# A four-chunk, two-layer transformer kernel: PSUM banks named step by step, folds as steps of their own, products of zeros at the start, and a new step list

## The reference, cut to what matters

```
layer 0:  xn   = layernorm(x)
          attn = causal softmax attention of xn with one head: q = xn Wq, k = xn Wk (both 1024 wide), v = xn Wv, out Wo
          ffn  = mixture over the top 2 of 8 experts; an expert is relu(xn wi + bi + xn A[e] B[e]) wo + bo,
                 the gate's logits are xn gate_w + gate_b
          x1   = x + attn * silu(ffn)
layer 1:  xn1  = layernorm(x1)
          attn = causal differential attention, 16 heads, two softmaxes per head, rms norm of each head, Wo
          ffn  = the top 8 of 32 experts (silu gate, up, down, 64 wide) and a shared expert
          out  = x1 + attn * silu(ffn)
```

## Time and profile before

| | us |
|---|---|
| runs | 492.76, 493.83, 493.89 |
| profiled execution, its time | 493.67 |
| profiled execution, its span (first to last instruction) | 491.9 |
| PE busy | 455.2 (93%) |
| DVE busy | 398.6 (81%) |
| ACT busy | 281.6 (57%) |
| POOL busy | 269.6 (55%) |

### The profile page before, as it was taken

The page is one execution under the profiler, slowest core; times in us unless marked ns, Lnnn a source line. Parts: engine busy times, 40 slices in busy tenths (PEclk is TensorE's granted clock), DMA queues, the critical chain, the costliest instruction groups (busy, mean ns, idle before and its releaser), DMA issues.

```text
span 491.9 us, 8510 instructions
## 1 busy us (share of the span) xinstructions
PE 455.2 (93%) x3072; PEld 219.5 (45%) x3072; DVE 398.6 (81%) x812; ACT 281.6 (57%) x456; POOL 269.6 (55%) x237
## 2 busy tenths in 40 slices
PE   2999888889999999999999999999889998989995
PEld 2755447434444345453454444544334453423332
DVE  1634457999998988899999978978999999986785
ACT  2264673446767635738876445556776537467640
POOL 6322360235554775547763459636675865546982
PEclk9999997999999999999999999999999999999998
DMA  7900059786952710232569643025592662204201
GB/s 277 338 14 0 22 182 194 127 142 182 234 111 76 127 18 4 73 84 65 176 181 168 111 62 91 1 65 171 178 172 43 121 98 77 58 5 113 59 2 43
DMA packets 54754, 52.44 MB, mean 107 GB/s; under 512 B 5080, under 2 KB 44344, under 8 KB 54072
## 3 DMA queue, kind: packets, MB, share of 16 engines
q1 hardware_dynamic: 54712, 51.90, 44.2%
HBM read 37.47 MB, written 13.89 MB: 104 GB/s over the span
## 4 chain that ended last, share of the span: by engine, by line
PE 73%; DVE 18%; ACT 3%; issue 2%; POOLq 1%; DMA 1%; POOL 1%; SPq 0%; DVEq 0%; ACTq 0%
PE bank L785 10%; PE bank L776 9%; PE bank L797 8%; PE scores L816 8%; PE bank L871 5%; DVE nmax L1335 3%; PE scores L711 3%; PE scores L702 3%; PE scores L726 3%; PE scores L705 3%; PE scores L810 3%; PE scores L750 3%; DVE h L1311 3%; PE bank L876 2%; DVE h L1318 2%
## 5 line engine op out<-in xcount | busy, mean ns | idle before, releaser
L1136 POOL TENSOR_TENSOR gb<-gb,wb 128x512 f32<-128x512 f32 x64 | 84.3, 1318 | 94.3 <-ACT gb L1024 76.3
L1039 ACT ACTIVATE pk<-scores 128x1024 f32<-128x1024 f32 x96 | 95.3, 1023 | 38.9 <-PE scores L816 38.7
L1129 POOL TENSOR_SCALAR_AFFINE_SELECT pk<-pk 128x512 f32<-128x512 f32 (+1 forms) x96 | 82.1, 864 | 39.8 <-ACT pk L1039 39.3
L1335 DVE TENSOR_REDUCE nmax<-scores 128x8 f32<-128x1024 f32 x64 | 76.4, 1216 | 7.7 <-PE scores L816 7.0
L1021 ACT ACTIVATE gt<-bank,bgh 128x512 f32<-128x512 f32 (+1 forms) x68 | 46.7, 687 | 62.5 <-PE bank L776 50.7
L785 PE MATMUL bank<-xnt,wu 128*128 128x512 f32 x128 | 68.3, 615 | 2.3 <-DVE h L1318 2.2
L776 PE MATMUL bank<-xnt,wg 128*128 128x512 f32 x128 | 69.4, 624 | 0.0
L797 PE MATMUL bank<-h,wd 128*128 128x512 f32 x128 | 66.5, 617 | 0.0
L1311 DVE SCALAR_TENSOR_TENSOR h<-gt,gb 128x512 f32<-128x512 f32 x64 | 57.8, 903 | 3.4 <-PE bank L797 3.1
L1318 DVE SCALAR_TENSOR_TENSOR h<-bank,bu,h 128x512 f32<-128x512 f32 x64 | 48.1, 751 | 10.8 <-PE bank L785 8.8
L1140 POOL TENSOR_TENSOR orms<-oms,minus_half 128x32 f32<-128x32 f32 x8 | 44.7, 5585 | 10.3 <-DVE oms L1365 10.3
(11 more groups left out here) (262 smaller groups left out, 711.1 us busy)
## 6 DMA issues: line engine op xcount, KB each, us to landing
wb<-wt_scratch SPq DMA_DIRECT2D x64, 256.0 KB, 4.2
parts_scratch<-parts SPq DMA_DIRECT2D x16, 384.0 KB, 3.0
qa<-parts_scratch SPq DMA_DIRECT2D x32, 192.0 KB, 4.9
ka<-parts_scratch SPq DMA_DIRECT2D x32, 192.0 KB, 5.9
parts_scratch<-parts SPq DMA_DIRECT2D x16, 256.0 KB, 3.1
parts_scratch<-parts SPq DMA_DIRECT2D x16, 128.0 KB, 2.8
ha<-in_wkq SPq DMA_DIRECT2D x1, 1024.0 KB, 4.8
wb<-in_wvo SPq DMA_DIRECT2D x1, 1024.0 KB, 7.5
```

The source lines that it names most:

```text
L1039: A(dst.rearrange("p (h m) q -> p m h q", m=2), pairs[pair_of(step)][:, :, :].rearrange("p m (h q) -> p m h q", q=cols), ACT.Exp, scale=SC ...
L1129: pool.affine_select(out=dst, in_=dst, compare_op=ALU.is_ge, fill=0.0, base=0, pattern=[[0, heads], [1, P]], channel_multiplier=-1).then_i ...
L1136: pw(gb[:, c % 2, :], gb[:, c % 2, :], wb[:, k % 2, j % 2, :], ALU.mult).then_inc(s_ga_done, 1)
L1335: V.tensor_reduce(dst, src, AX, ALU.max, negate=True).then_inc(s_nmax_done, 1)
```

## The change

1. PSUM becomes one tensor of eight banks. The list names for each step the first bank that it uses (`max/0/0/0/0@1` takes banks 1 and 2, `gate/0@5` bank 5). Bank 7 stays with `down`. A step waits for whichever steps last held its banks (`holders`, `banks_free`). `gate`, `up`, `values` and the rest no longer have banks of their own.
2. The folds are steps, `foldk/0` and `foldv/0`. On PE `foldk` stands ahead of the first transposes; on ACT its copy to `mt` stands ahead of `scale0/0`.
3. DVE fills `fth` (128x512, f32) with zeros first, and PE multiplies it by itself three times into bank 7 before it waits for anything else.
4. The gate's weights lie beside the factors A in one tile `lag` (136 columns). One product per 128 tokens gives both the logits and xn A, in step `keys0`, over two banks; the 8 matmul instructions a chunk for the logits alone (L648) are gone. `keys0` now holds its banks until `um` is done, and `inner0` holds the products with `mt` and `vo`.
5. The list is new. No instruction is added or removed by that, only moved.

Core of the diff (the same renaming of banks in every engine's part is left out, as are the two lists):

```diff
+ONE_BANK = ("foldk", "foldv", "turn0", "turn1", "router1", "fin", "minus", "values", "weights1", "out1", "gate", "up")
+ACC = 7
...
+def holders(steps, first):
+
+    last, before = {}, {}
+    for step in steps:
+        if step in first:
+            banks = range(first[step], first[step] + (1 if step[0] in ONE_BANK else 2))
+            before[step] = list(dict.fromkeys(last[k] for k in banks if k in last))
+            last.update((k, step) for k in banks)
+    return before
...
-    load/0 load/1 norm0/0 scale0/0 turn0/0 norm0/1 keys0/0 router0/0 inner0/0 picks0/0 scale0/1 scores0/0 hidden0/0
+    load/0 load/1 foldk/0@5 norm0/0 scale0/0 norm0/1 turn0/0@1 keys0/0@3 foldv/0@2 router0/0 scale0/1 inner0/0@5
...
+WARM = 3
...
-        la = sb("la", [P, E0 * R0])
+        lag = sb("lag", [P, E0 * R0 + E0])
+        la, gate_w = lag[:, 0:E0 * R0], lag[:, E0 * R0:]
...
+        def banks_free(pe, step):
+
+            for kind, c, *rest in HELD_BEFORE.get(step, ()):
+                if kind == "max":
+                    pe.wait_ge(s_nmax_done, unit(c, *rest) + 1)
+                elif kind == "score":
+                    pe.wait_ge(s_pk_done, unit(c, *rest) + 1)
...
+                elif kind == "gate" and c % STEPS < PAIRS:
+                    pe.wait_ge(s_gate_act, 2 * c + 2)
+                elif kind in ("gate", "up"):
+                    pe.wait_ge(s_h_done, c + 1)
...
+            pe.wait_ge(s_zeros, 1)
+            for _ in range(WARM):
+                mm(psum[:, ACC, :], fth[:, 0:P], fth[:, :], start=True, stop=True)
             pe.wait_ge(s_consts_ready, N_CONSTS)
...
+                if name == "foldk":
+                    pe.wait_ge(s_kq_in, 16)
+                    fold((name, c), kq_room, s_mt_done)
...
                     for k in range(TILES):
-                        last = mm(two[:, k * E0:(k + 1) * E0], xnt_of[side(c)][:, k * P:(k + 1) * P], gate_w[:, :], start=(k == 0), stop=True, skip_group_check=True)
+                        last = mm(inner(c)[:, k, 0:E0 * R0 + E0], xnt_of[side(c)][:, k * P:(k + 1) * P], lag[:, :],
+                                  start=(k % 2 == 0), stop=True, skip_group_check=True)
...
+            V.memset(fth[:, :], 0.0).then_inc(s_zeros, 1)
             dve.wait_ge(s_consts_ready, N_CONSTS)
```

More of the change, by code:

```diff
@@ L68 @@
 STEPS = PAIRS + 1
-FRONT = ("load", "norm0", "scale0", "turn0", "keys0", "router0", "inner0", "scores0", "picks0", "probs0", "hidden0",
+FRONT = ("foldk", "foldv", "load", "norm0", "scale0", "turn0", "keys0", "router0", "inner0", "scores0", "picks0", "probs0", "hidden0",
          "hidden1", "out0", "back0", "norm1", "scale1", "turn1", "router1", "choose1", "queries1", "keys1", "store", "values1",
          "weights1")
-RING = ("turn0", "keys0", "inner0", "scores0", "picks0", "probs0", "hidden0", "hidden1", "out0", "turn1", "router1",
-        "queries1", "keys1", "values1", "max", "score", "fin")
@@ L142 @@
-""")
-TAKERS = [step for step in PROGRAM if step[0] in RING]
-USERS4 = [step for step in PROGRAM if step[0] in BANK4]
-RANK = {step: n for n, step in enumerate(TAKERS)}
-RANK4 = {step: n for n, step in enumerate(USERS4)}
+    steps, first = [], {}
+    for token in text.split():
+        name, _, number = token.partition("@")
+        step = tuple(int(x) if x.isdigit() else x for x in name.split("/"))
+        steps.append(step)
+        if number:
+            first[step] = int(number)
+    return steps, first
@@ L163, in sem @@
             return ctx.enter_context(nc.semaphore(name))
-        pairs = [ctx.enter_context(nc.psum_tensor(f"scores{n}", [P, 2, 512], F32)) for n in range(2)]
-        single = [ctx.enter_context(nc.psum_tensor(f"bank{n}", [P, 512], F32)) for n in range(4, 8)]
-        bank = [pairs[0][:, 0, :], pairs[0][:, 1, :], pairs[1][:, 0, :], pairs[1][:, 1, :]] + [s[:, :] for s in single]
+        psum = ctx.enter_context(nc.psum_tensor("banks", [P, 8, 512], F32))
         ident = sb("ident", [P, P])
@@ L443, in side, with held, one_bank, two_banks @@
             return int(c == 1)
-        def pair_of(step):
-            if step[0] == "back0":
-                return RANK["out0", step[1]] % 2
-            return RANK[step] % 2
+        def held(step):
+            return BANK["out0", step[1]] if step[0] == "back0" else BANK.get(step, 0)
+        def one_bank(step):
+            return psum[:, BANK[step], :]
+        def two_banks(step):
+            return psum[:, BANK[step]:BANK[step] + 2, :]
+        def inner(c):
+            return two_banks(("keys0", c)).rearrange("p n (k s) -> p (n k) s", s=2 * P)
         def group(c, b, g):
@@ L842, in _ @@
                     query, key = ((0, 0), (P, P), (P, 0))[u]
-                    last = scores(pair_of(step), b, query, P, qa, ka, MROWS, GH * g, key, P, u < 2)
+                    last = scores(held(step), b, query, P, qa, ka, MROWS, GH * g, key, P, u < 2)
                     last.then_inc(s_max_ps, 1)
@@ L881, in _ @@
                     for f in range(2):
-                        last = mm(bank[4], wo1s[:, f, :], oct_[:, f, :], start=(f == 0), stop=(f == 1))
+                        last = mm(one_bank(step), wo1s[:, f, :], oct_[:, f, :], start=(f == 0), stop=(f == 1))
                     last.then_inc(s_s1_ps, 1)
@@ L894, in _, with front @@
             A = nc.scalar.activation
-            def front(name, c, pair):
+            def front(name, c, first):
                 if name == "scale0":
@@ L1006, in _ @@
                 if kind in FRONT:
-                    front(kind, c, pair_of(step) if kind in RING or kind == "back0" else 0)
+                    front(kind, c, held(step))
                 elif kind == "setup":
```

405 lines of the change are left out of this document (194 added, 211 removed).

## The result

Before 493.86 us (492.76 to 494.44, 4 runs), after 480.12 us (479.14 to 480.30, 4 runs), ratio 0.9726 with a 95% interval of 0.9703 to 0.9749. The changed kernel was run once more beside the last experiments: 480.94 us against 492.38, ratio 0.9761 (0.9735 to 0.9787). By these two ratios the change is worth 11.8 to 13.5 us. I had said 482.0 us. The profiled execution took 479.14 us, its span is 477.4: 14.5 less than 493.67 and 491.9. It is the fastest of its four.

What follows compares the result with a forecast made beforehand. It took PE to bound the long part, 105 to 480 us, with DVE close behind. 3.0 + 2.5 + 2.0 + 0 + 3.2 + 1.0 = 11.7 us off 493.7 gave 482.0 us, own range 478.5 to 485.0, 8 in 10 475 to 489.

Steps and rivals of the forecast that it cites:

- Start, 3.0 us: Kernel start: zeros, early folds and the second chunk's early scales and transposes bring 3.0 us.
- my two cases: Kernel start: 3.0 us gained with the clock up, 1.0 us with the low clock through the fold.
- C: Rival at the start: the fold runs at the low clock and the start gives nothing; 485 us, chance 0.14.
- Logits, 2.5 us: Logits inside the factors' product: 8 instructions a chunk go; chunks 1 to 3 save 2.5 us together, 0.8 to 3.5.
- Chunk 0's tail, 2.0 us: End of chunk 0: PE's waits at back0/0 for ACT and probs0/1 for DVE both go, 2.0 us.
- To the first maxima, net 0: Between chunk 1's layer 0 and first maxima: clock falls, PE arrives 3 us later with 3 us done ahead; net 0.
- The new list, 3.2 us for fewer changes: Long part: 23 fewer bf16-to-f32 changes at 0.19 us, 4.4 us less PE time, of which 3.2 us taken.
- Banks, 1.0 us: Long part: new bank assignment changes PE's bank waits, 1.0 us of gain, ends 8 less and 8 more.
- D: Rival: max and score steps waiting for slow gate, up or values banks hold all of PE; 497 us, chance 0.09.
- my sign of being wrong: PE's max and score rows wait on gate, up or values for over 10 us in sum.
- A: Rival: PE closes half its 10.7 us of gaps and the clock stays up before the maxima; 474 us, chance 0.17.
- B: Rival: DVE takes over in the long part, so the 3.2 and 1.0 are not seen; 486.2 us, chance 0.22.

Runs made afterwards that it cites:

- control: The changed kernel once more, unaltered, beside the last experiments: 480.94 us, ratio 0.9761 to the kernel before.
- more_changes: Changed kernel with 23 wd products moved later, so PE goes from bf16 to f32 steps 122 times instead of 99: 487.95 us.
- late_v: Changed kernel with POOL's two fills of v moved behind the second chunk's power: 480.81 us, ratio 0.9774 to the kernel before.
- old_order_free: Changed kernel with the old order of steps and banks chosen freely from 0 to 6 by estimated hold times: 523.75 and 530.86 us.
- keep_warm: Changed kernel with one more product of zeros behind each of the first chunk's 12 first maxima: 482.69 us, ratio 0.9796 to the kernel before.
- scores_later: Changed kernel with the third chunk's first-layer scores behind the first three maxima, in banks 2 and 3: 483.63 us, ratio 0.9831 to the kernel before.
- old_list: Changed kernel with the old order of steps and the old banks, all else as changed: 500.94 us, ratio 1.0132 to the kernel before.
- fold_later: Changed kernel with the first fold behind the transposes of the first chunk's xn: 482.66 us, ratio 0.9784 to the kernel before.
- logits_twice: Changed kernel with the four small logits products made again behind each chunk's factors' product: 484.37 us, ratio 0.9866 to the kernel before.
- both: Changed kernel with zeros behind the first chunk's first maxima and the first fold behind the transposes: 481.15 us, ratio 0.9779 to the kernel before.

## Why the prediction held, step by step

**Start, 3.0 us: right in this execution, and less in others.** hidden0 starts 3.16 us sooner. But in the control it starts at 23.38, 1.3 us sooner: the value lies between my two cases or beyond, by where the clock falls. That the profiled execution had the cheap fall is luck. The steps: fold before 9 us in less than 3, yes; xn from 8.62; `umt` ended at 20.74, I had 21.5. POOL's fill began at 10.32, not 10.9: the fold was done sooner than I had it, and xn at 10.25. What I called C needed a fold at the lower clock, and in after and the control it took 2.02 and 1.95 us; C's time of 485 us was not met either. The clock did fall again about a gap of PE, at one of two places. In after, more_changes, late_v and old_order_free it fell at 11.2 to 12.5 us, in or behind the gaps that follow the first fold; in the control, keep_warm, scores_later and old_list at 19.8 to 20.9 us, behind the wait for `um` of 2.1 to 2.6 us, and in fold_later at 17.9 us, within that wait, there 3.3 us; in logits_twice and in the run both at neither, though the latter had that wait too, with 3.3 us. The Trainium skill ("TensorE: Matmul & The Clock Gate", section "HAM oscillation — how this bites in real kernels") says that waits between bursts of matmuls can bring the clock down, and the traces agree in nine of these eleven profiles. But my price for it, 2.0 us wherever it falls, was wrong: with the fall at 12.2 us hidden0 starts at 21.52, without any (both) at 21.61, with the fall at 20.3 us at 23.38.

**Logits, 2.5 us: right as far as shown.** Chunk 3's 0.8 is what logits_twice shows in the long part; the sum of 3.4 to 4.3 there includes the spread of the start and of the first maxima. Chunk 2's part was not shown by itself.

**Chunk 0's tail, 2.0 us: right.** Both waits (0.93 and 1.24) are gone. From hidden0/0 to hidden0/1 PE needed 23.04 instead of 26.82 us, 3.8 less: 2.2 for the waits, 0.8 for the logits, 0.3 for a wait at probs0/0 that is gone too, and 0.4 for turn0/1, which only moved ahead of hidden0/0 and so belongs to the start.

**To the first maxima, net 0: near in sum by luck, wrong in its parts.** I expected the clock to fall near 75 us and PE to arrive 3 us later than its lead. The gap was there (1.67 us) but the clock stayed up, so that `gate/0`, `gate/1` and `scores0/2` fitted into what the lower clock had cost. The lead was larger than the 5.8 us that I had: the products of keys1/0 with `wk` started at 59.39 instead of 66.34 us, 6.9 sooner. 5.8 of it arrived at DVE's first maximum. Then 2.1 us were lost between the first and the 13th maximum: DVE's idle time there grew from 1.0 to 3.6 us, 1.3 of it at the maximum that waits for the bank of ACT's exponentials. I had no term for that. The work done ahead gave back 2.7 us later.

**The new list, 3.2 us for fewer changes: the term that was mis-sized.** 369.8 - 359.1 = 10.7 us in the long part. 2.7 of it is work done ahead (by their starts: 8 matmul instructions of `scores0/2` 1.42, 8 of the transposes of `picks0/2` 0.98, masks 0.26), 0.8 the logits. PE's busy time fell by 9.0, so 5.5 remain for the changes of kind; more_changes measured 5.7 for as many. I had taken the price on the f32 product alone (0.19); the products beside it pay too. And I had cut the term by PE's share of the chain, 73%. more_changes shows that nothing is to be cut: all of it reached the end.

**Banks, 1.0 us: about right.** Idle time of PE in that stretch fell by 1.7 us. D's mechanism is real in old_order_free and small here (3.2 us of such waits; my sign of being wrong was 10).

**Sum.** -5.8 to DVE's first maximum, +2.1 to the 13th, -10.8 to the power, 0 behind it: -14.5, as measured between the two profiled executions. Against this my 11.7 lacks 2.3 for the changes, 0.7 for idle time and 1.1 for the lead at keys1/0, and it has 1.4 too much between there and the 13th maximum. In the control the sum is -3.8, +2.4, -10.8: -12.2. So part of the forecast's nearness is luck: with the clock falling late, too small a term for the changes and too large a one for the start cancel. Of the rivals, A got the direction of half its case (idle time -1.7 where it had -5; the clock stayed up ahead of the maxima), B is refuted by more_changes.

What stays open: how much of the order's gain the freely named banks alone make possible, what decides where the clock falls, and why DVE's short operations on the maxima are long in some executions.

## What to carry to other kernels

Count the changes between bf16 and f32 products in an order of work: in this kernel, where PE is the bound, each cost 0.25 us, and none of it was hidden. An edit that makes a step hold its banks longer must be priced together with the rule that hands the banks out; here the merged product, the early folds and the zeros lost 6.5 us with the old order and rule (ratio 1.0132), and together with the new list the whole won 12 or more. And a dip of the clock has no price of its own: ask which work stands under it, and take more than one profile before a start is credited with 2 us.
